# Self attention and feed forward in one program: the last attention moved into a neighbouring product, the last output product by row tiles

## The reference, cut to what matters

```python
x = x + cross_attention(layernorm(x), ctx)            # ctx: 8 x 1601 x 2048
h = layernorm(x)
q, k, v = h @ w_q, h @ w_k, h @ w_v                   # 32 query heads, 8 key heads, of 128
x = x + causal_attention(q, k, v) @ w_o               # w_o: 4096 x 2048
h = layernorm(x)
gate = softmax over the 16 best of 64 router scores   # (h @ Wq_w.T) @ keys.T
z = (h @ A_w.T) * gate, each gate over 8 columns      # 512 wide
x = x + 2 * z @ B_w.T
```

## Time and profile before

| | us |
|---|---|
| median of three runs (1852.74 to 1854.44) | 1854.04 |
| the profiled execution, its own time | 1853.19 |
| its span, first to last instruction | 1851.3 |
| PE busy | 1718.7 |
| DVE, ACT, POOL busy | 719.5, 753.1, 856.6 |
| mean granted TensorE clock | 0.969 |

### The profile page before, as it was taken

How to read it: one execution, slowest core, us unless ns; L and a number is a source line. 1 busy time by engine, 2 the same in 40 slices (tenths; PEclk the granted TensorE clock), 3 DMA queues, 4 the chain that set the end, 5 groups by cost and what they waited for, 6 DMA issues and landing times. The chain is left out here.

```text
span 1851.3 us, 21688 instructions
## 1 busy us (share of the span) xinstructions
PE 1718.7 (93%) x8781; PEld 1421.0 (77%) x8781; DVE 719.5 (39%) x1088; ACT 753.1 (41%) x936; POOL 856.6 (46%) x300
## 2 busy tenths in 40 slices
PE   4899999999999954999999999999999999978999
PEld 3788888888888833887887878878878888756677
DVE  3666758577685676010211202202022030135523
ACT  2677877777778842222131121222212212211321
POOL 0488777877778832334424333333342433312010
PEclk8999999999999976999999999999999999979999
DMA  9155565556555423232332233223223232211113
GB/s 318 38 193 178 184 202 176 189 190 194 175 187 191 126 80 114 73 87 91 91 91 91 83 97 91 68 94 87 91 91 91 91 91 84 98 46 49 46 69 114
DMA packets 178351, 219.20 MB, mean 118 GB/s; under 512 B 4160, under 2 KB 102464, under 8 KB 176224
## 3 DMA queue, kind: packets, MB, share of 16 engines
q1 hardware_dynamic: 178288, 218.32, 37.4%
HBM read 209.92 MB, written 8.39 MB: 118 GB/s over the span
## 5 line engine op out<-in xcount | busy, mean ns | idle before, releaser
L853 POOL TENSOR_TENSOR sa_w_lo<-sa_raw,sa_w_hi 128x2048 fp32r<-128x2048 f32 x80 | 367.8, 4598 | 621.0 <-ACT sa_w_hi L867 621.0
L375 POOL TENSOR_TENSOR xa_nat_lo<-xa_raw_a,xa_nat_hi 128x1024 fp32r<-128x1024 f32 (+1 forms) x112 | 267.4, 2409 | 129.5 <-ACT xa_nat_hi L389 129.5
L525 DVE TENSOR_TENSOR xa_ct_lo<-xa_ps_t,xa_ct_hi 128x833 fp32r<-128x833 f32 (+1 forms) x256 | 252.9, 988 | 185.4 <-ACT xa_ct_hi L414 102.3
L705 PE MATMUL sa_ps_mm<-h_hi,sa_w_hi 128*128 128x512 f32 x768 | 302.6, 394 | 1.4 <-DVE h_lo L928 1.4
L707 PE MATMUL sa_ps_mm<-h_hi,sa_w_lo 128*128 128x512 f32 x768 | 299.1, 389 | 0.0
L706 PE MATMUL sa_ps_mm<-h_lo,sa_w_hi 128*128 128x512 f32 x768 | 299.0, 389 | 0.0
L993 DVE TENSOR_TENSOR rows<-rows,sa_ps_mm 128x512 f32<-128x512 f32 x128 | 88.0, 687 | 493.4 <-PE sa_ps_mm L707 493.4
L414 ACT ACTIVATE xa_ct_hi<-xa_ps_t 128x833 fp32r<-128x833 f32 (+1 forms) x256 | 215.0, 840 | 152.0 <-PE xa_ps_t L575 105.1
L867 ACT ACTIVATE sa_w_hi<-sa_raw 128x2048 fp32r<-128x2048 f32 x80 | 153.0, 1913 | 286.5 <-PE sa_ps_mm L707 286.5
L375 POOL TENSOR_TENSOR xa_nat_lo<-xa_raw_b,xa_nat_hi 128x1024 fp32r<-128x1024 f32 x88 | 210.9, 2404 | 55.7 <-ACT xa_nat_hi L389 52.9
L705 PE MATMUL sa_ps_mm<-sa_w_hi,sa_o_hi 128*128 128x512 f32 x512 | 204.0, 398 | 6.9 <-ACT sa_q_t L899 4.8
(11 more groups left out here) (173 smaller groups left out, 2294.6 us busy)
## 6 DMA issues: line engine op xcount, KB each, us to landing
xa_raw_a<-in_ctx SPq DMA_DIRECT2D x32, 1536.0 KB
xa_raw_b<-in_ctx SPq DMA_DIRECT2D x32, 1536.0 KB, 7.1
sa_raw<-in_L_attn_w_q SPq DMA_DIRECT2D x32, 1024.0 KB, 6.0
sa_raw<-in_L_attn_w_o SPq DMA_DIRECT2D x32, 1024.0 KB, 5.0
sa_raw<-in_L_attn_w_k SPq DMA_DIRECT2D x8, 1024.0 KB, 5.4
sa_raw<-in_L_attn_w_v SPq DMA_DIRECT2D x8, 1024.0 KB, 5.3
xa_xq<-in_x SPq DMA_DIRECT2D x8, 512.0 KB, 5.4
xa_raw_a<-in_ctx SPq DMA_DIRECT2D x32, 128.0 KB
```

Source lines behind the costliest of these rows:

```text
L375: pool.tensor_tensor(nat_lo[0:p, u % NAT, :, :], src, nat_hi[0:p, u % NAT, :, :].bitcast(F32), ALU.subtract).then_inc(nat_pool, 1)
L525: i = dve.tensor_tensor(ct_lo[:, t % RING, 0:w], ps_t[:, t % RING, 0:w], ct_hi[:, t % RING, 0:w].bitcast(F32), ALU.subtract)
L705: pe.matmul(out, hi, mov_hi, start=first, stop=False)
L853: pool.tensor_tensor(w_lo[:, n, :], raw[:, n, :], w_hi[:, n, :].bitcast(F32), ALU.subtract).then_inc(w_lo_done, 1)
```

## The change

The two programs become one, `decoder`, with all tensors at fixed offsets that share memory over time, and one PSUM tensor. What it does:

1. The loop has six turns; the projections of the last group and the output product of group 6 are written out behind it. The scores of the last group come ahead of that product, the transposes of its probabilities after its fourth tile, the first half of its values ahead of its last two tiles, the second half behind it. The exp and the softmax on ACT and DVE move with them.
2. The last output product goes by row tiles, with column chunks in the order 0, 1, 3, 2. Chunks 2 and 3 are loaded into `normed` ahead of the last group's loads; chunk 0 sits in the ring, chunk 1 in the last quarter of `h_hi`/`h_lo`.
3. Under it go the four transpose slots of the first A_w item, and for row tiles 0 to 2 the chain of the layer norm (one a row tile, three Newton steps), the normalisation (columns 0 to 1023 on ACT, the rest on DVE) and the transposes.
4. The first `down` product is split: columns 0 to 383 ahead of the transposes of the last row tile and three slots of the next item, columns 384 to 511 behind the router product.
5. The router weights and keys are loaded and transposed in turn 0, between its first two projections. The gates' transpose and expansion come later in the second `down` product. The hi/lo pairs of A_w and B_w turn through three places in place of two.
6. `rows_rsqrt` has three Newton steps in place of four (both calls in self attention).

```diff
-    for _ in range(4):
+    for _ in range(3):
...
+def row_rsqrt_steps(dve, bn, mv, w, r):
+    yield dve.bn_aggr(mv[:, r, :], bn[:, r, :, :])
+    yield from rsqrt_steps(dve, w[:, :, r], mv[:, r, 1:2])
...
+ENDING_WO = [0, 1, 3, 2]
+EARLY = 3 * P
...
 # SyncE
+            turns(sp, turn)
+            sp.wait_ge(wq_done, 1)
+            sp.dma_start(normed[:, 1, :].rearrange("p (h n) -> p h n", h=HG), chunk(3)).then_inc(fourth_in, 16)
+            sp.dma_start(normed[:, 0, :].rearrange("p (h n) -> p h n", h=HG), chunk(2)).then_inc(third_in, 16)
+            turn(LAST)
+            for c in range(2):
+                sp.wait_ge(w_lo_done, RING_ITEMS + c - 1)
+                sp.dma_start(raw[:, c, :].rearrange("p (h n) -> p h n", h=HG), chunk(c)).then_inc(w_in[c], 16)
...
 # GpSimd, behind the ring's loop
+            pool.wait_ge(w_hi_done, RING_ITEMS - 1)
+            low(0)
+            pool.wait_ge(fourth_hi_done, 1)
+            pool.wait_ge(pt_done, GROUPS)
+            pool.tensor_tensor(fourth_lo[:], normed[:, 1, :], fourth_hi[:].bitcast(F32),
+                               ALU.subtract).then_inc(fourth_lo_done, 1)
...
+            low(1)
...
+            low(0)
+            pool.wait_ge(w_hi_done, RING_ITEMS + 2)
+            pool.tensor_tensor(strip(h_lo), sixteen(raw[:, 1, :]), strip(h_hi).bitcast(F32),
+                               ALU.subtract).then_inc(w_lo_done, 1)
...
 # ScalarE
+            heads_out(GROUPS, 0)
+            heads_out(GROUPS, 1)
+            act.wait_ge(third_in, 16)
+            act.wait_ge(wo_bank, WO_BEFORE)
+            act.activation(w_hi[:, 1, :], normed[:, 0, :], ACT.Copy).then_inc(third_hi_done, 1)
...
+            for r in range(RT):
+                act.wait_ge(ln_ready, r + 1)
...
+                act.activation(normed[:, 0, 0:D // 2], rows[:, r, 0:D // 2], ACT.Identity, bias=shift[:, r:r + 1],
+                               scale=rs_w[:, 0, r:r + 1]).then_inc(norm_act, 1)
+                for q in range(QUADS):
+                    evacuate("h", r, q)
...
 # VectorE
+            softmax_shift(GROUPS)
+            for n in range(NCOL * RT):
+                add_rows(LAST, n, n % RT, n // RT)
+                if n == 1:
+                    softmax_scale(GROUPS)
+                if n == NCOL * RT - 3:
+                    heads_low(GROUPS, 0)
...
+            heads_low(GROUPS, 1)
+            dve.wait_ge(third_hi_done, 1)
+            dve.tensor_tensor(w_lo[:, 1, :], normed[:, 0, :], w_hi[:, 1, :].bitcast(F32),
+                              ALU.subtract).then_inc(third_lo_done, 1)
+            for r in range(RT):
+                for i, c in enumerate(ENDING_WO):
+                    n = NCOL * r + i
+                    add_rows(GROUPS, n, r, c)
+                    dve.wait_ge(wo_added, 1 + WO_BEFORE + n + 1)
+                    ins = dve.bn_stats(row_bn[:, r, c, :], rows[:, r, c * 512:(c + 1) * 512])
+                    if r == 0:
+                        evacuate("w", 0, i)
+                    elif i in (1, 2):
+                        evacuate("h", r - 1, 2 * i - 2)
+                        evacuate("h", r - 1, 2 * i - 1)
+                link(ins)
+                layernorm(r)
...
 # TensorE
+            project_group(LAST)
+            attend_scores(GROUPS)
+            for c in range(NCOL):
+                for r in range(RT):
+                    if c == NCOL - 1 and r == 2:
+                        attend_values(GROUPS, 0)
+                    times_w_o(LAST, c, r)
+                if c == 0:
+                    probs_transpose(GROUPS)
+            attend_values(GROUPS, 1)
...
+            for r in range(RT):
+                for i, c in enumerate(ENDING_WO):
+                    ending_w_o(r, i, c)
+                    if r == 0:
+                        t_slot("w", 0, i)
+                    elif i in (1, 2):
+                        t_slot("h", r - 1, 2 * i - 2)
+                        t_slot("h", r - 1, 2 * i - 1)
...
+            pe.wait_ge(wo_added, 1 + WO_BEFORE + NCOL * RT)
+            for c in range(DC):
+                down_part(0, c, slice(0, EARLY))
+            for q in range(QUADS):
+                t_slot("h", RT - 1, q)
+            for q in range(3):
+                t_slot("w", 1, q)
...
+            for c in range(DC):
+                i = down_part(0, c, slice(EARLY, ROWS))
+            i.then_inc(z_done, 1)
+            t_slot("w", 1, 3)
```

More of the change, by code:

```diff
@@ L909, in turn @@
                     split(g, n + 2)
-                for c in range(n_wo if n_proj else 2):
-                    split(g, n_proj + c + 2)
+            def turn(g):
+                projections(g)
+                for c in range(kind(g)[1]):
+                    split(g, NP + c + 2)
             turns(act, turn)
+            projections(LAST)
+            exponentials(GROUPS)
+            split(LAST, NP + 2)
+            probs_t(GROUPS)
+            act.wait_ge(fourth_in, 16)
+            act.wait_ge(s_done, GROUPS)
@@ L915, in _ @@
+            evacuate("w", 2, 2)
+            for a in range(ZC):
+                act.wait_ge(gx_done, a + 1)
+                act.activation(gates[:, a, :], ps_r[:, a % 2, :], ACT.Copy).then_inc(gx_out, 1)
+            z_high(0)
+            evacuate("w", 2, 3)
+            z_high(1)
+            for m in range(3, ITEMS):
+                for q in range(4):
+                    evacuate("w", m, q)
+                if m - 1 < ZC:
+                    z_high(m - 1)
         @block.vector
@@ L955, in _, with softmax_shift @@
             dve.wait_ge(mask_ready, 3)
-            def turn(g):
-                n_proj, n_wo = kind(g)
-                if not n_wo:
-                    dve.memset(s_inv[:], 0.0).then_inc(wo_added, 1)
-                    return
-                last = isinstance(g, int) and g == GROUPS
+            def softmax_shift(g):
                 here = base + SOFTMAX_LINKS * (g - 1)
-                def step(ins, n):
-                    ins.then_inc(chain, 1)
-                    dve.wait_ge(chain, here + n)
@@ new lines, in _ @@
+            link(i)
+            for r in range(RT):
+                i = dve.match_replace(out=rest[:, 1, r, :], in_to_replace=best[:, r, 8:16], in_values=rest[:, 0, r, :],
+                                      imm_value=-3.0e38)
+            link(i)
+            link(dve.tensor_tensor(chosen[:], rest[:, 1, :, :], sc[:], ALU.not_equal))
+            dve.wait_ge(exp_done, 1)
+            link(dve.tensor_tensor(chosen[:], chosen[:], expo[:], ALU.mult))
+            link(dve.tensor_reduce(g_sum[:], chosen[:], AX.X, ALU.add))
@@ L1001, in _ @@
+            for c in range(NCOL):
+                for r in range(RT):
+                    n = RT * c + r
+                    dve.wait_ge(o_done, n + 1)
+                    part = rows[:, r, c * 512:(c + 1) * 512]
+                    dve.tensor_tensor(part, part, ps_mm[:, n % 2, :], ALU.add).then_inc(o_added, 1)
+                    if ZC + c + 1 < ITEMS:
+                        evacuate("w", ZC + c + 1, r)
         @block.tensor
@@ L1108, in turn @@
+                project(g, 5)
+                if not n_wo:
+                    pe.wait_ge(wq_ready, 1)
+            def turn(g):
+                project_group(g)
+                if kind(g)[1]:
                     for c in range(NCOL):
-                        times_w_o(g, c)
+                        for r in range(RT):
+                            times_w_o(g, c, r)
             turns(pe, turn)
-EXPERTS, RANK, RD, TOP = 64, 8, 16, 16
-NZ = EXPERTS * RANK
-ZC = NZ // P
-SCALING = 2.0
-ITEMS = ZC + NCOL
@@ L1433, in gate_transpose @@
+            i.then_inc(z_done, 1)
+            t_slot("w", 1, 3)
+            pe.wait_ge(q_ready, 1)
+            pe.wait_ge(wq_hi, 1)
+            for r in range(RT):
+                i = pe.matmul(ps_r[:, 1, r * EXPERTS:(r + 1) * EXPERTS], qr_t[:, r * P:(r + 1) * P], keys_t[:],
+                              start=True, stop=True)
+            i.then_inc(sc_done, 1)
             def gate_transpose():
```

810 lines of the change are left out of this document (419 added, 391 removed).

## The result

The changed kernel takes 1811.9 us (median of four runs, 1807.08 to 1815.27), where the kernel before took 1854.24 in the same rounds: a ratio of 0.977, 95% interval 0.9747 to 0.9794. That is 42 us faster. The prediction had the sign and 30 of them; at 1824.1 us it was 12 too high, and the time lies outside its range of 1818 to 1830. The profiled execution took 1812.09 us (span 1810.3), against the 1823.3 of the sum.

The account below looks back on a forecast made before the run. PE bounds the kernel (busy 93%), its late waits set by row work on DVE and ACT. Terms of 153.1 for 183.22 us, less 0.2, gain 29.9: 1853.19 becomes 1823.3, plus 0.85 for the median: 1824.1 us, range 1818 to 1830.

Parts of the forecast that it names:

- 192 matmuls at clock 1.00, 0.2339 us each: Output product in a turn of the loop: 44.91 us on PE with nothing between the matmuls, kept as its price.
- what lies behind it I take as unchanged: Everything behind the reordered stretch 1585.24 to 1768.46 (183.22 us) was to keep its time.
- the ending: Last output product with sixteen slots and row work under it: 52.4 us, then 1.0 waiting for the last add.
- the 128-column matmuls: Second part of the first `down` product, behind the router: 48 matmuls at 0.175 us, 8.4 us, range 5.5 to 11.2.
- the front: Turn 0: seventeen small transposes moved there cost 1.4 us, fewer Newton steps save twice 0.6; net +0.2.
- The last attention: Last group's attention together with the output product of group 6: 51.8 us in place of 67.97, 16.2 us saved.
- The weight chunks: Splits and loads of the last output product's weights: ready in time, five microseconds spare, nothing charged.
- The first `down`: After the last add: 384-column matmuls 8.5 us, hiding the last row tile's chain (5.7); seven slots 4.7; router product 7.5.
- Rival A: The clock falls once or twice around the seven slots before the router product: 1.5 to 3 us, 1826 to 1827; chance 0.13.
- B: Row work doesn't fit under a row tile of the last output product: PE waits 9 to 10 us, 1833.5; chance 0.12.
- C: Fixed places in memory make waits that give the whole gain back: 1853 to 1855; chance 0.03.
- D: Transposes between the last output product's tiles pull the clock down throughout it: slower, up to 1874; chance 0.03.

Follow-up runs that it names:

- the second trace: The changed kernel, nothing edited, profiled and timed again: median of five runs 1816.9 us, ratio 0.9777 to the kernel before.

## Why the prediction was wrong

*The step that failed* is the price of a matmul of the output product, "192 matmuls at clock 1.00, 0.2339 us each", carried over as fixed, and with it "what lies behind it I take as unchanged" for all that the reordering doesn't touch. The 0.2339 belongs to the place of o in memory, which the change moved: 0.2273 (43.65 / 192) is the rate after. This is 7.6 us in the loop, 1.2 in "the product of group 6 its 44.91", 0.4 in "192 matmuls, 44.91" of the ending and at most the 0.3 that the rest is faster when both have a dip: 9 to 10 of the 11 that are missing. The other differences nearly cancel: 3.1 us for the 128-column matmuls and 1.6 for the dip of the clock in the rest on one side, 2.6 in the front and 0.8 in the ending on the other. The prediction itself named the sign, "if the turns of the loop change their length", and didn't ask what of the diff could do it, though the fixed offsets of every tensor are in it. And the kernel before already had two rates for one shape: a record of its projections, whose stationary operand starts at a multiple of 512, has 389 ns, one of its output product 396 (above).

*The 128-column matmuls* are the term that was mis-sized: 0.1106 us each, 5.31 in all, just under the lower bound (5.5). The scores' row was the nearer one, and the middle between it and the fp32 row had no reason of its own. 3.1 us.

*The last attention*: right. 50.60 for 51.8, and the difference is the rate (51.80 with o 32 bytes off).

*The weight chunks*: right, nothing waits for them.

*The ending*: 53.80 for 53.4 with the last add. It holds two errors that nearly cancel: at the old rate it takes 54.17, 0.8 more than forecast, and the rate gives 0.4 back. Beside the bare product the sixteen slots and their waits take 54.17 - 44.91 - 1.0 = 8.3 at the old rate where 7.5 was charged. The three waits for the normalised rows are 1.2 in the changed kernel, twice the 0.6. (The terms of the latency that the prediction lists, 0.2, 1.4, 2.9 and 1.05, add up to 5.55, not 5.7.)

*The first `down`*: 384 columns, seven slots and router are right to 0.2 each, and the split hides a chain that costs 5.9 when it is bare.

*The front*: the transposes cost 1.5 for 1.4 charged, and the chains are 1.0 shorter. The rest of its +2.6 is 1.3 of clock and a cross attention that ends 1 us later in this trace.

*Rival A* was given 0.13, and it is what the second trace has in part: a dip of the clock, 3.1 us, though from the scores of group 7 on and not around the seven slots. *B* didn't come: three waits of 0.4. *C* didn't come. *D* didn't: in 1631.03 to 1684.83 sixteen slots lie among the matmuls at 1.00. The Trainium skill, page "TensorE: Matmul & The Clock Gate", section "Part 4: PE-mode transpose", has it that the full clock does not engage for transposes. Where they are mixed into a dense stream of products this trace shows no loss from them. Where the row work stands bare the clock is 0.60, but there PE is also idle for 18.6 of 29.69 us, so that run doesn't tell the two apart.

## What to carry to other kernels

Put the stationary operand of a product at a start address that is a multiple of 256 bytes and look whether the start-to-start time of its matmuls changes: here a padding of 480 bytes, alone, was worth 8.8 us in seven turns, of 1855. Whenever a change moves tensors, take no rate of a matmul as fixed; two rates for one shape in one profile are a thing to explain before it is used. And cover a chain of row work with products that don't need it: the three covers here are worth 15, 23 and 3 us when undone one at a time, part of it the clock that falls in the gap.

## What was not expected of the hardware

- The matmuls of the output product, whose stationary operand starts 32, 64 or 128 bytes past a multiple of 256, start 0.233 to 0.234 us apart and have records of 395 to 396 ns, against 0.2273 us and 389 ns at a multiple of 256. Where transposes and waits lie between the matmuls, less of it shows: 0.4 us in the ending, 0.7 in the rest with `up`, in place of 1.3. In the cross attention, moving its stationary operands to a multiple of 512 took off only 2 of 396 ns.
- Matmuls of 128, 256 and 384 columns with new weights each start 0.11, 0.12 and 0.17 us apart: 128 columns are hardly cheaper than 256.
- The clock fell to half for several us inside and behind 32 matmuls of 64 columns (0.57 over 8 us in which PE was busy without a gap, a wait of 0.69 us shortly before), in one of two executions of the same program. In the other the same wait and matmuls stand at a clock of 1.00.
